# Layer norm and projections of an attention stage: some of ScalarE's time for z, another order on VectorE, projections in halves

## The chip, the cores and the metric

The kernel runs on the 8 cores of one Trainium2 chip. No core talks to another; each computes half of the rows of one of 4 sequences. The time is device microseconds of the slowest core, and the figure quoted is a median over runs.

## The reference

x is 4 sequences of 4096 rows with 1024 columns. Two pre-norm residual layers follow one another:

```
z   = layernorm(x)
q,k,v = z @ Wq, z @ Wk, z @ Wv            # 1024 -> 64 each
att = softmax(q @ k^T, axis=1)            # over the rows i of q, for each key column
x1  = x + tile(att @ v, 16)               # 64 -> 1024
z1  = layernorm(x1);  zp = z1 shifted by one row
r   = sigmoid((mu_r z1 + (1-mu_r) zp) @ Wr)
k   = (mu_k z1 + (1-mu_k) zp) @ Wk
y   = x1 + r * (relu(k)^2 @ Wv2)
```

The softmax runs over queries, so each key needs the exponentials of all 4096 queries. A core therefore makes z, q and k of all 4096 rows, and outputs only for its own 2048.

## The kernel before

Every engine has its program written out by hand, in a fixed order, with semaphores between them. The edited part is the first stage, which feeds the exponentials.

*Tiles and chunks.* The 4096 rows are 32 tiles of 128. x of a tile comes by DMA from SyncE's queue (`load_x`, line 327) into one of 8 slots. A slot is used again when z of the tile 8 before is made. VectorE computes the statistics of a tile with `stats(i)`: `stats_a` (first half, line 492), `stats_b` (second half, line 495, and the aggregate, line 497). GpSimd takes tiles in pairs: `scale` makes the negated mean, variance plus epsilon, and its power -0.5 for both (lines 402, 404, 407), and `apply` makes z = (x - mean) * rstd in bf16 for each (line 417). GpSimd counts tiles done in `G_Z`.

*z transposed.* Tiles 0 to 15 are transposed on TensorE (`T(i)`, line 810) into PSUM, and copied to `zT` by ScalarE for tiles 0 to 7 (`t_evac`, line 1122) and by VectorE for 8 to 15 (line 505). Tiles 16 to 31 are transposed by DMA from SyncE's queue (`turn_z`, line 336), in order with the loads of x.

*Chunk steps.* Four tiles are a chunk n of 512 rows, 0 to 7. `QK(n)` is the projection, 8 matmuls (line 827); `qk_evac(n)` on VectorE casts it to bf16 (line 510); `SW(n)` swaps the halves q and k on TensorE (line 839) and `sw_evac(n)` casts the result (line 514); `MX(n)` scores each key against a sample of 128 queries (line 851), and `mx(n)` takes the maximum as the shift of the exponential (line 528). For each two chunks `VP(sc)` projects the values (line 863, 16 matmuls), `v_evac` casts (line 518), `VT(sc)` transposes (line 873), `vt_evac` copies (line 522).

*Units.* A unit is a block of scores, 128 keys by 512 or 1024 queries. There are 136, numbered here from 0, in groups: a group may start when the swapped cast and the maximum of its chunk are there. Units 0 to 3 need chunk 0, 4 to 11 chunk 1, 12 to 19 chunk 2, 20 to 39 chunk 3, 40 to 47 chunk 4, 48 to 63 chunk 5, all others chunk 7. TensorE scores a unit with one or two matmuls (`fill`, lines 886 and 890) into a buffer in PSUM (2 buffers until unit 19, then 3), and ScalarE exponentiates it (`exps`, line 1139) and frees the buffer. `scores(n)` in TensorE's order means the next n units. From unit 64 on TensorE also adds up the output (line 899), between units.

The order of TensorE is a hand-written list in which `T`, `QK`, `SW`, `MX`, `VP`, `VT` and `scores` alternate; VectorE has a list of its own:

```
            mx(0)
            stats(10)
            stats(11)
            stats(12)
            t_evac(8)
            stats(13)
            qk_evac(1)
...
            v_evac(0)
            stats(15)
            qk_evac(2)
```

After the last exponential ScalarE loads the table of the square root (line 1148), and the second part follows: attention output, second layer norm (`ln2_apply`, line 1168, an Identity activation with a scale and a bias for each row), and the matmuls of the second layer (lines 1037, 1058, 1080).

Of the kernel before, what the change touches and what calls it, by code (L numbers as in the profile page):

```python
# [23 lines left out]
NA = 8  # L24
NF2 = 20
# [41 lines left out]
def build_program():  # L67
# [58 lines left out]
    with ctx:  # L126
# [12 lines left out]
        rstd = e(nc.sbuf_tensor("rstd", [128, TT], F32))  # L139
        so = e(nc.sbuf_tensor("so", [128, TOWN], F32))  # L140
# [108 lines left out]
        G_Z = sem("G_Z")  # L249
        P_T = sem("P_T")  # L250
# [45 lines left out]

        def own_p(kt):
            return P0[:, kt, :] if kt < 16 else Prot[:, kt % 4, :]
# [24 lines left out]
        def _(sy):  # L323
            def load_x(i):
                if i >= 8:
                    sy.wait_ge(G_Z, i - 7)
                sy.dma_start(out=xst[:, i % 8, :],
                             in_=x_in[i * 128:(i + 1) * 128, :]).then_inc(D_X[i % 8], 16)

            def turn_z(i):  # L330
                sc = i // 8
                sy.wait_ge(G_Z, i + 1)
# [59 lines left out]
        def _(g):  # L392
# [36 lines left out]
            g.wait_ge(G_Z, TT)  # L429
# [55 lines left out]
        def _(v):  # L485
# [56 lines left out]
            stats(12)  # L542
            t_evac(8)
            stats(13)
            qk_evac(1)
            t_evac(9)
            t_evac(10)
            sw_evac(1)
            mx(1)
            t_evac(11)  # L550
            stats(14)
            v_evac(0)
            stats(15)
            qk_evac(2)
            stats_a(16)
            vt_evac(0)
            mx(2)
            sw_evac(2)
            stats_b(16)
            t_evac(12)  # L560
            stats_a(17)
            t_evac(13)
            stats_b(17)
            t_evac(14)
            t_evac(15)
            stats(18)
            qk_evac(3)
            stats_a(19)
            sw_evac(3)
            mx(3)  # L570
            stats_b(19)
            stats(20)
            stats(21)
            v_evac(1)
            stats(22)
            vt_evac(1)
# [222 lines left out]
        def _(t):  # L799
# [3 lines left out]
            def T(i):  # L803
                t.wait_ge(G_Z, i + 1)
# [9 lines left out]
            def QK(n):  # L814
# [11 lines left out]
                for ct in range(CT):  # L826
# [4 lines left out]
                ins.then_inc(P_QK, 1)  # L831

            def SW(n):
                t.wait_ge(V_QK, n + 1)
                if n % 2:
                    t.wait_ge(V_SW, n)
                elif n:
                    t.wait_ge(V_VT, n // 2)
# [18 lines left out]
            def VP(sc):  # L857
                if sc == 0:
                    t.wait_ge(D_WV, 16)
                t.wait_ge(V_SW, 2 * sc + 2)  # L860
                for ct in range(CT):
# [52 lines left out]
            t.wait_ge(D_ID, 16)  # L914
            T(0)
# [11 lines left out]
            scores(2)  # L927
            QK(1)
# [3 lines left out]
            T(10)  # L932
            SW(1)
            MX(1)
            T(11)
            scores(1)
            VP(0)
            QK(2)
            scores(1)
            VT(0)  # L940
            scores(1)
            MX(2)
            SW(2)
# [4 lines left out]
            scores(1)  # L948
# [3 lines left out]
            scores(2)  # L952
            QK(3)
            scores(2)
# [3 lines left out]
            VP(1)  # L958
            scores(3)
            VT(1)  # L960
            scores(8)
            QK(4)
            scores(3)
# [3 lines left out]
            QK(5)  # L967
            scores(3)
# [3 lines left out]
            VP(2)  # L972
            scores(3)
            VT(2)
            scores(7)
            QK(6)
            scores(3)
            SW(6)
            MX(6)
            scores(3)  # L980
            QK(7)
            scores(3)
# [3 lines left out]
            VP(3)  # L986
            scores(2)
# [128 lines left out]
        def _(sc):  # L1116
# [25 lines left out]

            for i in range(NA):
                t_evac(i)
            for u_ in range(NU):
# [131 lines left out]
```

## Time and profile before

| | |
|---|---|
| median of 3 runs | 395.83 us (395.75 to 396.2) |
| profiled execution | 396.79 us, span of its slowest core 394.9 us |
| spans of the 8 cores | 388.7 to 394.9 us |
| TensorE busy | 312.6 us, 79% of the span |
| ScalarE busy | 225.9 us, 57% |
| VectorE busy | 224.5 us, 57% |
| GpSimd busy | 116.5 us, 29% |

The span runs from the first to the last instruction of a core. The shares are averages over parts with different limits: in the first 200 us ScalarE carries the exponentials, in the rest TensorE is busy nearly all the time. So the timelines and waits of the first part say more than the table. PE is TensorE, DVE VectorE, ACT ScalarE, POOL GpSimd.

### The profile page before, as it was taken

To read this page: it belongs to the slowest core of one execution; us is meant where nothing else is said; L and a number is where in the kernel's file an instruction comes from. 1 tells how busy PE (TensorE), PEld (TensorE's weight loads), DVE (VectorE), ACT (ScalarE), POOL (GpSimd) and SP (SyncE) were. 2 spreads that over 40 slices of the span, in tenths; PEclk is the share of its full clock that TensorE was granted. 3 is DMA by queue.
4 is the path that set the end of the run, shared out by engine and by line. 5 is a ranking of instruction groups with operands and counts; after the bars stand their busy time and mean duration, and the time that the engine had idled before them with its cause. 6 is when DMAs were issued, how large, how long until landed. Compare 5 with 4: busy or idle time off the path is not lost.

```text
span 394.9 us, 6253 instructions; the slowest of 8 cores (388.7 to 394.9 us)
## 1 busy us (share of the span) xinstructions
PE 312.6 (79%) x1938; PEld 143.1 (36%) x1938; DVE 224.5 (57%) x440; ACT 225.9 (57%) x354; POOL 116.5 (29%) x161
## 2 busy tenths in 40 slices
PE   0377986696878767776526989799999999999994
PEld 0333332231224434342223334244444444444441
DVE  2787789337236631112188976879278836781045
ACT  1252289989889999999916409302860267014610
POOL 1887457607304885068470021001000000000000
PEclk9997798866695888886555989899999999999999
DMA  7999547896596789991002004131322214130014
GB/s 179 291 317 287 144 140 188 147 290 102 101 173 188 250 176 181 183 266 79 1 2 46 7 2 81 27 147 67 55 53 106 110 33 75 69 144 2 0 53 160
DMA packets 42368, 48.58 MB, mean 123 GB/s; under 512 B 33248, under 2 KB 33504, under 8 KB 41952
## 3 DMA queue, kind: packets, MB, share of 16 engines
q1 hardware_dynamic: 41472, 41.44, 37.5%
q0 software_dynamic: 864, 6.75, 10.7%
q8 instruction: 16, 0.26, 0.3%
q14 instruction: 16, 0.13, 0.1%
HBM read 38.68 MB, written 8.39 MB: 119 GB/s over the span
## 4 chain that ended last, share of the span: by engine, by line
PE 52%; ACT 20%; DVE 12%; issue 11%; DMA 2%; POOL 1%; DVEq 0%; SPq 0%; ACTq 0%; POOLq 0%
PE F L1080 14%; PE F L1037 10%; PE F L1058 10%; PE tf L827 6%; PE F L886 6%; ACT Prot L1139 5%; ACT junkL L1139 5%; ACT junk L1139 4%; ACT P L1139 3%; DMA xst<-x_in 2%; DVE xr L667 2%; PE acc L899 2%; PE tf L863 1%; PE tx L810 1%; DVE dxk L677 1%
## 5 line engine op out<-in xcount | busy, mean ns | idle before, releaser
L886 PE MATMUL F<-qk 64*128 64x512 bf16 x136 | 59.2, 456 | 34.4 <-ACT Prot L1139 11.0
L1058 PE MATMUL F<-dxk,wk 128*128 128x512 bf16 x256 | 58.6, 386 | 1.8 <-DVE dxk L677 1.7
L1080 PE MATMUL F<-wv,ka 128*128 128x512 bf16 x256 | 57.5, 387 | 2.9 <-ACT ka L1186 2.9
L1178 ACT ACTIVATE rr<-F 128x1024 bf16<-128x1024 f32 x16 | 16.4, 1023 | 73.6 <-PE F L1037 73.6
L1037 PE MATMUL F<-wr,xr 128*128 128x512 bf16 x256 | 57.8, 384 | 0.6 <-DVE xr L667 0.6
L890 PE MATMUL F<-qk 64*128 64x512 bf16 x120 | 54.8, 474 | 0.0
L1139 ACT ACTIVATE P<-F,negm 128x1024 bf16<-128x1024 f32 (+1 forms) x40 | 37.2, 948 | 19.5 <-PE F L886 15.6
L1139 ACT ACTIVATE junk<-F,negm 128x1024 bf16<-128x1024 f32 x32 | 39.8, 1255 | 3.1 <-PE F L890 3.1
L1139 ACT ACTIVATE junkL<-F,negm 128x1024 bf16<-128x1024 f32 x32 | 39.9, 1281 | 0.0
L417 POOL TENSOR_SCALAR zst<-xst,nmean,rstd 128x1024 bf16<-128x1024 f32 x32 | 38.0, 1194 | 3.6 <-POOL rstd L407 3.6
L1139 ACT ACTIVATE Prot<-F,negm 128x1024 bf16<-128x1024 f32 x32 | 39.0, 1346 | 0.0
L1080 PEld LDWEIGHTS F<-wv,ka 128*128 128x128 bf16 x256 | 25.4, 99 | 34.5 <-issue 5.5
L1058 PEld LDWEIGHTS F<-dxk,wk 128*128 128x128 bf16 x256 | 25.3, 99 | 34.4 <-issue 6.1
L886 PEld LDWEIGHTS F<-qk 64*128 64x128 bf16 x136 | 12.4, 97 | 68.8 <-issue 66.4
L781 DVE TENSOR_TENSOR tmp<-F,rr 128x1024 f32<-128x1024 f32 x15 | 18.4, 1224 | 32.8 <-PE F L1080 32.5
L1037 PEld LDWEIGHTS F<-wr,xr 128*128 128x128 bf16 x256 | 25.2, 99 | 31.7 <-issue 2.7
L606 DVE TENSOR_REDUCE ell<-ellp 128x1 f32<-128x4 f32 (+1 forms) x32 | 4.9, 155 | 49.5 <-ACT junkL L1139 49.5
L439 POOL TENSOR_TENSOR fold<-x 128x512 f32<-128x512 f32 x16 | 20.2, 1265 | 33.9 <-DMA x<-x_in 33.9
L667 DVE SCALAR_TENSOR_TENSOR xr<-dxk,mu,z1T 128x256 bf16<-128x256 bf16 (+1 forms) x80 | 28.3, 427 | 2.3 <-PE F L1037 1.0
L492 DVE BATCH_NORM_STATS2 bnst<-xst 128x6 f32<-128x512 f32 x32 | 21.8, 680 | 8.3 <-DMA xst<-x_in 8.3
L827 PE MATMUL tf<-zT,wqk 128*128 128x512 bf16 x64 | 24.3, 549 | 1.4 <-ACT zT L1122 1.3
L810 PE MATMUL tx<-idsw,zst 128*128 128x128 bf16 x128 | 11.7, 249 | 17.1 <-POOL zst L417 15.9
(103 smaller groups left out, 446.7 us busy)
## 6 DMA issues: line engine op xcount, KB each, us to landing
xst<-x_in SPq DMA_DIRECT2D x32, 512.0 KB, 7.1
x<-x_in SPq DMA_DIRECT2D x16, 512.0 KB, 5.3
y_out<-x SPq DMA_DIRECT2D x15, 512.0 KB, 2.6
wr<-wr_in POOLq DMA_DIRECT2D x1, 2048.0 KB, 16.2
wk<-wk_in POOLq DMA_DIRECT2D x1, 2048.0 KB, 18.2
wv<-wv_in POOLq DMA_DIRECT2D x1, 2048.0 KB, 21.0
y_out<-x SPq DMA_DIRECT2D x2, 256.0 KB, 2.1
wqk<-wqk_in POOLq DMA_DIRECT2D x1, 256.0 KB, 9.2
```

What stands on the lines that cost most here:

```text
L417: g.tensor_scalar(zst[:, i % 8, :], xst[:, i % 8, :], nmean[:, i:i + 1], rstd[:, i:i + 1], ALU.add, ALU.mult).then_inc(G_Z, 1)
L439: g.tensor_tensor(fold[:, 0:512], x1[:, t_, 0:512], x1[:, t_, 512:1024], ALU.add).then_inc(G_XF, 1)
L492: v.bn_stats(bnst[:, i % 4, 0:6], xst[:, i % 8, 0:512]).then_inc(V_ST, 1)
L667: ins = v.scalar_tensor_tensor(xr[:, ct, o:o + w], dxk[:, q % 2, ct, o:o + w], mu[:, ct:ct + 1], z1T[:, ct, c0 - 1:c0 + w - 1], ALU.mult, ...
L781: v.tensor_tensor(tmp[:, :], F[(8 + j) % 3][:, :], rr[:, j, :], ALU.mult).then_inc(V_TMP, 1)
L827: ins = t.matmul(tf[0][:, :], wqk[:, ct, :], zT[:, (n // 2) % 2, ct, (n % 2) * 512:(n % 2 + 1) * 512], start=(ct == 0), stop=(ct == CT - 1 ...
L886: t.matmul(f[:, 0:512], qk2[0:64, kt * 128:(kt + 1) * 128], qk1[0:64, i0:i0 + 512], start=True, stop=True, skip_group_check=True, tile_pos ...
L890: t.matmul(f[:, 512:1024], qk1[64:128, kt * 128:(kt + 1) * 128], qk2[64:128, i0 + 512:i0 + 1024], start=True, stop=True, skip_group_check= ...
L1037: ins = t.matmul(f[:, hh * 512:(hh + 1) * 512], xr[:, ct, j * 128:(j + 1) * 128], wr[:, ct, hh * 512:(hh + 1) * 512], start=(ct == 0), sto ...
L1058: ins = t.matmul(F[k_ % 3][:, dd * 512:(dd + 1) * 512], wk[:, ct, dt * 128:(dt + 1) * 128], dxk[:, q % 2, ct, :], start=(ct == 0), stop=(c ...
L1080: ins = t.matmul(F[(8 + j) % 3][:, hh * 512:(hh + 1) * 512], ka[:, dt, j * 128:(j + 1) * 128], wv2[:, dt, hh * 512:(hh + 1) * 512], start= ...
L1139: sc.activation(dst, F[f_of[u_]][:, 0:w], AF.Exp, bias=negm[:, kt:kt + 1], accum_out=ellp[:, ell_col[u_]:ell_col[u_] + 1]).then_inc(A_EXP, 1)
```

## The change

- ScalarE makes z of tiles 5, 11 and 15, as one Identity activation with scale rstd and bias -mean * rstd. GpSimd makes that bias (`nmr1`) after the scale of the pair, and leaves out the tile. The new `z_done(i)` says which semaphore and count stand for z of tile i; all who waited on `G_Z` use it. ScalarE does tile 5 after its fourth copy, tile 11 after exponential 3, tile 15 after exponential 16.
- VectorE's order: the steps of chunks 1, 2 and 3 move ahead of later statistics, the first cast of the values moves behind statistics 15.
- TensorE's order: all projections but the first, and the value projections, are in two halves of 4 of the 8 steps, with one unit between (`QK2`, `VP2`); the units between other steps are spread anew.

```
+AZT = [5, 11, 15]
...
+        def z_done(i):
+            if i in AZT:
+                return A_Z, AZT.index(i) + 1
+            return G_Z, i + 1 - sum(a < i for a in AZT)
...
                 scale(2 * h, 2, h)
+                if 2 * h + 1 in AZT:
+                    i = 2 * h + 1
+                    g.tensor_tensor(nmr1[:, i:i + 1], nmean[:, i:i + 1], rstd[:, i:i + 1],
+                                    ALU.mult).then_inc(G_NM, 1)
                 apply(2 * h)
-                apply(2 * h + 1)
+                if 2 * h + 1 not in AZT:
+                    apply(2 * h + 1)
```

VectorE's order from `mx(0)` on, before and after:

```
 stats 10 11 12, t_evac 8, stats 13     | stats 10 11, qk_evac 1, t_evac 8
 qk_evac 1, t_evac 9 10                 | sw_evac 1, mx 1, t_evac 9 10 11
 sw_evac 1, mx 1, t_evac 11, stats 14   | stats 12 13, qk_evac 2, stats_a 14
 v_evac 0, stats 15, qk_evac 2          | sw_evac 2, mx 2, stats_b 14, stats 15
 stats_a 16, vt_evac 0, mx 2, sw_evac 2 | v_evac 0, t_evac 12 13, vt_evac 0
 stats_b 16, t_evac 12, stats_a 17      | stats 16, t_evac 14 15, stats 17
 t_evac 13, stats_b 17, t_evac 14 15    | qk_evac 3, stats_a 18, sw_evac 3
 stats 18, qk_evac 3, stats_a 19        | mx 3, stats_b 18, stats 19 20
 sw_evac 3, mx 3, stats_b 19            | v_evac 1, stats 21, vt_evac 1
 stats 20 21, v_evac 1, stats 22        | stats 22 ...
 vt_evac 1, stats 23 ...                |
```

Units that TensorE has scored before each step, before and after:

```
 QK 1: 3 | 2   QK 2: 5 | 7    QK 3: 14 | 18  QK 4: 29 | 31
 QK 5: 38 | 40 QK 6: 52 | 53  QK 7: 58 | 58
 VP 0: 5 | 11  VP 1: 18 | 22  VP 2: 42 | 44  VP 3: 62 | 62
```

The halves on TensorE, and ScalarE's part:

```
+            def QK2(n):
+                QK(n, 0, 4)
+                scores(1)
+                QK(n, 4, CT)
+            def VP2(sc):
+                VP(sc, 0, 4)
+                scores(1)
+                VP(sc, 4, CT)
...
+            def apply(i):
+                sc.wait_ge(G_NM, AZT.index(i) + 1)
+                if i >= 8:
+                    sc.wait_ge(P_T, i - 7)
+                sc.activation(zst[:, i % 8, :], xst[:, i % 8, :], AF.Identity,
+                              bias=nmr1[:, i:i + 1], scale=rstd[:, i:i + 1]).then_inc(A_Z, 1)
-            for i in range(NA):
+            for i in range(4):
                 t_evac(i)
-            for u_ in range(NU):
+            apply(5)
+            for i in range(4, NA):
+                t_evac(i)
+            for u_ in range(4):
+                exps(u_)
+            apply(11)
+            for u_ in range(4, 17):
+                exps(u_)
+            apply(15)
+            for u_ in range(17, NU):
                 exps(u_)
```

The waits of `VP`, `SW` and `T` on semaphores are fitted to the new order; what they wait for in data is the same.

## Rows read from the trace of the kernel before

**Rows 1.** Spans and granted clock of the cores (us, share of full clock).

```profile
core 0: 394.9 us, clock 0.868
...
core 2: 394.1 us, clock 0.881
...
core 5: 388.7 us, clock 0.892
```

**Rows 2.** ScalarE's waits, 29 to 121 us (us in total, times, longest).

```profile
ACT P L1139 <- PE F L886: 15.6, 5, 5.7
ACT P L1139 <- PE F L890: 3.8, 4, 1.7
ACT junk L1139 <- PE F L890: 3.1, 2, 1.7
```

**Rows 3.** Timeline of ScalarE (start us, us, engine, line, operation, count, idle before).

```profile
28.61 1.02 ACT L1122 ACTIVATE zT<-tx 128x1024 bf16<-128x1024 bf16 x1 [0.30 <-PE tx L810]
...
63.66 0.69 ACT L1139 ACTIVATE P<-F,negm 128x512 bf16<-128x512 f32 x1
...
76.69 1.12 ACT L1139 ACTIVATE P<-F,negm 128x1024 bf16<-128x1024 f32 x1
...
77.78 1.13 ACT L1139 ACTIVATE P<-F,negm 128x1024 bf16<-128x1024 f32 x1
...
111.41 1.10 ACT L1139 ACTIVATE junk<-F,negm 128x1024 bf16<-128x1024 f32 x1
...
195.93 1.28 ACT L1148 ACT_TABLE_LOAD   x1
```

**Rows 4.** Timeline of VectorE, 37 to 61 us.

```profile
37.33 0.67 DVE L510 CAST qk<-tf 128x512 bf16<-128x512 f32 x1
...
39.10 0.68 DVE L514 CAST qk<-tf 128x512 bf16<-128x512 f32 x1
39.70 0.68 DVE L528 TENSOR_REDUCE negm<-tf 128x4 f32<-128x512 f32 x1
...
48.90 0.69 DVE L514 CAST qk<-tf 128x512 bf16<-128x512 f32 x1
...
58.86 0.68 DVE L528 TENSOR_REDUCE negm<-tf 128x4 f32<-128x512 f32 x1
...
60.25 0.21 DVE L497 BATCH_NORM_AGGREGATE ag<-bnst 128x2 f32<-128x12 f32 x1
```

**Rows 5.** Timeline of TensorE, projections 1, 5 and 7.

```profile
30.75 3.13 PE L827 MATMUL tf<-zT,wqk 128*128 128x512 bf16 x8
...
80.79 3.59 PE L827 MATMUL tf<-zT,wqk 128*128 128x512 bf16 x8
...
106.30 3.55 PE L827 MATMUL tf<-zT,wqk 128*128 128x512 bf16 x8 [0.16 <-issue]
```

**Rows 6.** Timeline of GpSimd, 46 to 107 us.

```profile
46.93 0.23 POOL L402 TENSOR_SCALAR nmean<-ag 128x2 f32<-128x2 f32 x1 [5.37 <-DVE ag L497]
...
47.61 0.70 POOL L407 TENSOR_TENSOR rstd<-vpe,mhalf 128x2 f32<-128x2 f32 x1
48.56 2.37 POOL L417 TENSOR_SCALAR zst<-xst,nmean,rstd 128x1024 bf16<-128x1024 f32 x2 [0.24 <-POOL rstd L407]
...
106.13 0.62 POOL L432 DMA_DIRECT2D wr<-wr_in  x1 [3.85 <-DMA zT<-zst]
```

**Rows 7.** Timeline of TensorE on core 5, projections 3, 5 and 7.

```profile
50.59 1.90 PE L827 MATMUL tf<-zT,wqk 128*128 128x512 bf16 x8
...
77.27 3.11 PE L827 MATMUL tf<-zT,wqk 128*128 128x512 bf16 x8
...
101.67 1.89 PE L827 MATMUL tf<-zT,wqk 128*128 128x512 bf16 x8 [0.16 <-issue]
```

**Rows 8.** Timeline of ScalarE in the second part.

```profile
207.85 1.24 ACT L1168 ACTIVATE z<-x,nmr,rstd 128x1024 bf16<-128x1024 f32 x1 [0.65 <-DVE nmr L657]
...
218.13 1.28 ACT L1178 ACT_TABLE_LOAD   x1 [3.11 <-PE F L1037]
```

More of the change, by code:

```diff
@@ L249, in build_program @@
         G_Z = sem("G_Z")
+        G_NM = sem("G_NM")
+        A_Z = sem("A_Z")
         P_T = sem("P_T")
@@ L541, in _ @@
             stats(11)
-            stats(12)
+            qk_evac(1)
             t_evac(8)
-            stats(13)
-            qk_evac(1)
+            sw_evac(1)
+            mx(1)
             t_evac(9)
             t_evac(10)
-            sw_evac(1)
-            mx(1)
             t_evac(11)
-            stats(14)
+            stats(12)
+            stats(13)
+            qk_evac(2)
+            stats_a(14)
+            sw_evac(2)
+            mx(2)
+            stats_b(14)
+            stats(15)
             v_evac(0)
-            stats(15)
-            qk_evac(2)
-            stats_a(16)
+            t_evac(12)
+            t_evac(13)
             vt_evac(0)
[L557 to L563, printed above, removed]
+            stats(16)
             t_evac(14)
             t_evac(15)
-            stats(18)
+            stats(17)
             qk_evac(3)
-            stats_a(19)
+            stats_a(18)
             sw_evac(3)
             mx(3)
-            stats_b(19)
+            stats_b(18)
+            stats(19)
             stats(20)
+            v_evac(1)
             stats(21)
-            v_evac(1)
+            vt_evac(1)
             stats(22)
-            vt_evac(1)
             stats(23)
@@ L825, in QK @@
                     t.wait_ge(V_MX, n)
-                for ct in range(CT):
+                for ct in range(a, b):
                     ins = t.matmul(tf[0][:, :], wqk[:, ct, :],
@@ L855, in MX, with VP @@
                 ins.then_inc(P_MX, 1)
-            def VP(sc):
+            def VP(sc, a=0, b=CT):
                 if sc == 0:
                     t.wait_ge(D_WV, 16)
-                t.wait_ge(V_SW, 2 * sc + 2)
-                for ct in range(CT):
+                t.wait_ge(V_SW, 2 * sc + 2 if sc else 3)
+                for ct in range(a, b):
                     for h in range(2):
@@ L926, in _ @@
             T(7)
-            scores(2)
-            QK(1)
+            scores(1)
+            QK2(1)
             scores(1)
@@ L931, in _ @@
             T(9)
-            T(10)
             SW(1)
             MX(1)
+            T(10)
+            scores(2)
             T(11)
             scores(1)
-            VP(0)
-            QK(2)
+            QK2(2)
+            scores(2)
+            SW(2)
+            MX(2)
             scores(1)
[L940 to L943, printed above, removed]
+            VP2(0)
             scores(2)
@@ L947, in _ @@
             T(13)
-            scores(1)
+            VT(0)
+            scores(2)
             T(14)
@@ L951, in _ @@
             T(15)
-            scores(2)
-            QK(3)
-            scores(2)
+            QK2(3)
+            scores(1)
             SW(3)
@@ L957, in _ @@
             scores(2)
-            VP(1)
+            VP2(1)
             scores(3)
             VT(1)
-            scores(8)
-            QK(4)
-            scores(3)
+            scores(5)
+            QK2(4)
+            scores(2)
             SW(4)
@@ L966, in _ @@
             scores(6)
-            QK(5)
-            scores(3)
+            QK2(5)
+            scores(2)
             SW(5)
@@ L971, in _ @@
             scores(1)
-            VP(2)
-            scores(3)
+            VP2(2)
+            scores(2)
             VT(2)
-            scores(7)
-            QK(6)
-            scores(3)
+            scores(6)
+            QK2(6)
+            scores(2)
             SW(6)
             MX(6)
-            scores(3)
-            QK(7)
-            scores(3)
+            scores(2)
+            QK2(7)
+            scores(2)
             SW(7)
@@ L985, in _ @@
             scores(1)
-            VP(3)
-            scores(2)
+            VP2(3)
+            scores(1)
             VT(3)
```

18 lines of the change are left out of this document (10 added, 8 removed).

## The prediction

> **What bounds the kernel now.** I read the spans of the cores first. The slowest core sets the metric, and core 0 is slowest with 394.9 us; core 2 is close, core 5 is 6.2 us shorter [rows 1]. Next I looked for where core 0 changes its pace. ScalarE's timeline shows exponentials of full units 1.09 us apart (76.69, 77.78) and the table load that follows the last of 136 at 195.93 [rows 3]. The rest, 199.0 us on core 0, holds none of the edited lines and begins with that load. So the question is only when the last exponential ends: ScalarE's work in the first part is fixed, and what can be saved is its idle time. The waits of ScalarE from 29 to 121 us say how much there is: 15.6 + 3.8 + 3.1 = 22.5 us, all on score matmuls [rows 2]. Most of it lies before unit 20, the first that needs chunk 3, which is exponentiated at 63.66 [rows 3].
>
> Why scores are late is seen in the other engines. VectorE handles chunk 1 at 37.33 (cast), 39.10 and 39.70 (maximum), though its projection began on TensorE at 30.75 and took 3.13 us: statistics stand in front in VectorE's order [rows 4, 5]. GpSimd waits 5.37 us for the statistics of tiles 14 and 15, which stand behind such steps too, and starts that pair at 46.93 [rows 6]. From chunk 4 on there is a second loop. Statistics 26 to 31 stand behind projection 5 on VectorE; GpSimd makes their z; the DMA transposes it; projection 7 waits for that. On core 0 projection 5 ends at 80.79 + 3.59 = 84.38 and projection 7 starts at 106.30, 21.9 us later [rows 5]. On core 5 it is 77.27 + 3.11 = 80.38 to 101.67, 21.3 us [rows 7]. That the last transpose is the tight end is shown by GpSimd's weight load, which waits 3.85 us for it until 106.13, just before projection 7 [rows 6]. This loop has nothing to gain from a lead of ScalarE unless projection 5 itself ends earlier.
>
> **The change, step by step, core 0.** Start times before are rows, new ones my sums.
>
> *Tile 5 on ScalarE.* An application there costs 1.24 us by the layer-2 ones of the same shape [rows 8]. It falls between copies that wait for projection 0, so it costs nothing; without that cover it would cost its 1.24. GpSimd saves half of 2.37 us a pair and pays for one product 128x1. No row shows that product: it lies between the 0.23 of the negation and the 0.70 of the power, and I take 0.3, as it is the plainer operation [rows 6]. The saving, about 0.9, goes into waiting for the next statistics. Nothing is gained here.
>
> *Chunk 1.* Before, projection 1 stood behind two units, the second waiting for the first exponential, and began at 30.75. Now one unit stands in front and the copy of tile 7 (28.61 + 1.02) releases it: 29.7. With one unit inside (0.6) it ends at 33.4. The cast follows at once (37.33 before), then one copy; the swap comes behind transposes 8 and 9; the swapped cast starts at 35.6, the maximum at 36.2 instead of 39.70. Lead 3.5 us.
>
> *Chunk 2.* Transposes 10 and 11 with their copies put projection 2 at about 39.1; it ends near 42.0, as do statistics 12 and 13. Its swapped cast starts at 43.4 instead of 48.90 [rows 4]. Tile 11 on ScalarE lies in idle time. Lead over 5 us.
>
> *Chunk 3 gives part back.* Statistics 15 end at 47.0, no earlier than the 46.9, where GpSimd started on them before. GpSimd has z of 14 by 50.1, but tile 15 now stands in ScalarE's order behind exponential 16, which ends at about 51.8: z at 53.0, against 48.56 + 2.37 = 50.9 [rows 6]. Behind that wait stand transpose 15, its copy, projection 3. On SyncE's queue the load of x 23 waits for z 15 as well, 2 us longer, with the DMA transpose of tile 16 behind it; z of 16 comes after that anyway, and x 23 is wanted some 15 us later, so this costs nothing. The maximum of chunk 3 starts at 58.7, where it started before (58.86). The lead of the units remains, since units 0 to 19 need chunks 0 to 2 only: unit 20 at 59.4 instead of 63.66, 4.2 us.
>
> *Projection 4.* Before, the statistics of 18 were half done and those of 19 ended at 60.25 + 0.21, right after the maximum. Now both stand almost wholly behind it, and 19 is done at 61.7 [rows 4]. GpSimd needs 50.93 - 46.93 = 4.0 for the pair [rows 6], with 0.2 to start 65.9, and by the 3.85 of the last tile z lands at 69.7. Thirty-one units are scored by then; exponential 30 ends near 70.5 after about 0.7 lost on the split value projection. At 1.2 GHz, 0.45 us a matmul as in projection 5 (3.59 for 8), half a projection is 1.8 and a unit 0.6. So unit 31 comes at 72.1 and unit 32 at 74.3, against 76.69 [rows 3]. Of the lead 2.4 is left.
>
> *Projection 5* now follows 40 units, where it followed 38: 2 x 1.09 later in ScalarE's count. Exponential 36 ends at 74.3 + 5 x 1.09 = 79.8, one unit 0.6, the projection 3.6 with 0.6 for the unit inside: end 84.6, against 84.38. The whole lead is eaten at this point. The split itself saves little: ScalarE gets one more unit (1.09) while TensorE needs 0.6 more, 0.5 per projection at the low clock. At 2.4 GHz, 1.89 a projection, it saves nothing, since three buffered units cover that already.
>
> *Projection 7.* The loop of 21.9 less 0.3, as the swap stands behind two units now, puts its start at 106.2. Unit 59 is the second after its first half. Low clock: 106.2 + 3.6 + 1.2 = 111.0, against 111.41. High clock: 106.2 + 1.9 + 0.75 = 108.85. Then ScalarE runs to the end without gaps, as from 111.41 on before. The sum is -0.4 to -2.6 us. Core 0 had the low clock in projection 7, core 5 the high one [rows 5, 7], so I take -1.7. Core 2, 0.8 us ahead in span, I take to follow core 0.
>
> The profiled execution took 396.79 us with a span of 394.9, and lies 0.96 above the median of 395.83. A span of 393.2 then stands for 395.1 in its own time and **394.1 us** for the median.
>
> *A rule to weigh.* No row shows Identity while the exponential table is active; the rows show Identity in the layer-2 part with the next load only at 218.13, 1.28 us, before the sigmoid [rows 8]. The Trainium skill (ScalarE: Activation LUTs, "Table sets: the hidden batching unit") says that cheap functions are in every set; by that three applications cost no load, and the sum stands. Were it not so, six loads of 1.28, two of them in idle time, would add up to 5 us.
>
> **The rivals.**
> (A) As above: the loop 5 to 7 gives back the lead. -0.4 to -2.6, 393.2 to 395.4. Chance 0.45.
> (B) The clock is high in projections 4 and 5 (1.9 instead of 3.6). Then unit 32 comes at 72.3, projection 5 ends near 80.5, projection 7 starts near 102, and unit 59 comes 5 to 7 us earlier: 389 to 391; with one of the two high, 391.5 to 393. For it: denser work before chunk 3. Against it: 3.59 and 3.11 on both cores [rows 5, 7], with TensorE waiting between units. Chance 0.22. The Trainium skill (TensorE: Matmul & The Clock Gate, "What's actually happening") says that activity releases the throttle; the added wait for z before projection 4 speaks by that for (A).
> (C) The whole lead goes: core 2 or a core with late tiles comes out at its old end. 395.1 to 396.6. Chance 0.11.
> (D) Slower. Tile 15 waits on ScalarE and statistics 14 to 19 stand further back on VectorE. On a core that is early now this is loss. Core 5 begins projection 3 at 50.59 [rows 7]; by the same links as above I get exponential 16 done there at 50.2, z of 15 at 51.4, its transpose and copy by 52.9, so 2.3 us later, and the loop carries most of it to the end. If core 0 pays the same, the time is 395.83 + 2.2 - 0.5 = 397.5. It decides where projection 3 begins more than 3 us later than by my sum. For it: the chain through exponential 16 has six links in my sum (unit 16, its exponential, z, transpose, copy, projection), each of which can slip. Against it: on core 0 the old wait of 5.37 us goes. Chance 0.20, and 0.02 more for table loads.
>
> **How the numbers follow.** A difference under 0.2%, 0.8 us, can't be told from none. A puts some 0.13 of its chance within that; C 0.09, and 0.01 on either side. Faster 0.32 + 0.22 + 0.01 = 0.55; same 0.13 + 0.09 = 0.22; slower 0.01 + 0.20 + 0.02 = 0.23. The range leaves out the best half of B and the worst of D: 390.3 to 397.2; for A alone it is 393.2 to 395.4.
>
> **What would show it.** Right: the maximum of chunk 1 near 36, the swapped cast of chunk 2 near 44, that of chunk 3 unmoved; unit 20 four microseconds earlier; a wait of ScalarE and TensorE before projection 4 that was not there; projection 5 ending where it did; projection 7 released by the DMA. Wrong: projections 4 to 6 near 2 us each (B), projection 3 after 57 (D), a table load between 20 and 60 us, or a slowest core in which x arrives later than here.

## The result, and the profile after

The changed kernel takes **398.22 us** (median of 5 runs, 396.96 to 400.24) against 395.83 of before: ratio 1.006, 95% interval 1.0039 to 1.0081. The prediction, 394.1 us with a range to 397.2, was wrong. It went the way of rival D, the one that said slower. The profiled execution took 398.22 us too. Medians here and below are over all executions of a kernel; ratios, intervals and core means leave out the few in which one die showed a lower clock and took longer.

The spans of the cores (us, granted clock):

```profile
core 0: 396.4 us, clock 0.877
...
core 2: 395.4 us, clock 0.885
...
core 5: 393.1 us, clock 0.880
```

Core 0 is 1.5 us longer than in [rows 1], core 5 is 4.4 us longer. It is not a matter of the slowest core alone: the mean span of the eight cores over the runs went from 391.8 to 394.0. I call this mean the core mean below; it scatters less than the slowest core. For the kernel before it was 391.7 to 391.8 in each of the four groups of experiments below. The changed kernel was timed in five executions and not again in those groups, so differences of core mean against its 394.0 can be off by some 0.3.

ScalarE's waits on core 0, 29 to 122 us (us in total, times, longest):

```profile
ACT P L1167 <- PE F L904: 8.4, 8, 1.6
ACT P L1167 <- PE F L908: 7.6, 6, 3.8
ACT junk L1167 <- PE F L908: 2.8, 3, 1.5
ACT junkL L1167 <- PE F L908: 1.1, 1, 1.1
ACT Prot L1167 <- PE F L908: 0.5, 1, 0.5
```

That is 20.4 us of waits on scores, 2.1 less than the 22.5 in [rows 2]. But ScalarE now also does two applications of 1.23 in this stretch, 2.5 us. Waits that shrink because the engine does other work are no gain. ScalarE's timeline, to be held against [rows 3]:

```profile
35.29 1.23 ACT L1175 ACTIVATE zst<-xst,nmr,rstd 128x1024 bf16<-128x1024 f32 x1
...
52.24 1.23 ACT L1175 ACTIVATE zst<-xst,nmr,rstd 128x1024 bf16<-128x1024 f32 x1
...
62.98 0.69 ACT L1167 ACTIVATE P<-F,negm 128x512 bf16<-128x512 f32 x1 [1.32 <-PE F L904]
...
77.76 1.11 ACT L1167 ACTIVATE P<-F,negm 128x1024 bf16<-128x1024 f32 x1 [0.78 <-PE F L908]
...
111.72 1.11 ACT L1167 ACTIVATE junk<-F,negm 128x1024 bf16<-128x1024 f32 x1
...
118.75 1.12 ACT L1167 ACTIVATE junkL<-F,negm 128x1024 bf16<-128x1024 f32 x1 [1.10 <-PE F L908]
...
197.74 1.28 ACT L1192 ACT_TABLE_LOAD   x1
```

Unit 20 is 0.7 us earlier than before, not 4.2. Unit 32 is already 1.1 later. The table load comes 1.8 us later. Behind it 198.7 us are left, 199.0 before: all of the loss lies in the first part, as argued. VectorE shows where the lead went (compare [rows 4]):

```profile
36.59 0.69 DVE L529 CAST qk<-tf 128x512 bf16<-128x512 f32 x1 [0.31 <-PE tf L857]
37.20 0.68 DVE L543 TENSOR_REDUCE negm<-tf 128x4 f32<-128x512 f32 x1
...
44.34 0.69 DVE L529 CAST qk<-tf 128x512 bf16<-128x512 f32 x1
...
60.12 0.69 DVE L525 CAST qk<-tf 128x512 bf16<-128x512 f32 x1 [3.08 <-PE tf L842]
...
62.15 0.68 DVE L543 TENSOR_REDUCE negm<-tf 128x4 f32<-128x512 f32 x1
...
65.02 0.21 DVE L512 BATCH_NORM_AGGREGATE ag<-bnst 128x2 f32<-128x12 f32 x1
```

The maximum of chunk 1 is 2.5 us earlier, the swapped cast of chunk 2 is 4.6 earlier, the maximum of chunk 3 is 3.3 later. VectorE stood idle for 3.08 us before the cast of chunk 3, and the releaser is TensorE's projection. Statistics 19, behind it in order, end at 65.2, where they ended at 60.5. TensorE (compare [rows 5]):

```profile
53.72 1.01 PE L824 MATMUL tx<-idsw,zst 128*128 128x128 bf16 x8 [1.45 <-ACT zst L1175]
55.78 1.86 PE L842 MATMUL tf<-zT,wqk 128*128 128x512 bf16 x4 [1.05 <-DVE zT L520]
...
58.12 1.89 PE L842 MATMUL tf<-zT,wqk 128*128 128x512 bf16 x4
...
84.04 1.86 PE L842 MATMUL tf<-zT,wqk 128*128 128x512 bf16 x4 [0.16 <-issue]
86.38 1.46 PE L842 MATMUL tf<-zT,wqk 128*128 128x512 bf16 x4
...
108.95 1.02 PE L842 MATMUL tf<-zT,wqk 128*128 128x512 bf16 x4 [1.79 <-DMA zT<-zst]
110.23 1.04 PE L842 MATMUL tf<-zT,wqk 128*128 128x512 bf16 x4
```

Before, projection 3 on this core was:

```profile
54.83 1.90 PE L827 MATMUL tf<-zT,wqk 128*128 128x512 bf16 x8
```

Now it begins at 55.78, one microsecond later. But four of its matmuls take 1.86, where all eight took 1.90: it runs at 1.2 GHz. With the unit between its halves it lasts 4.2 us. On all eight cores it lasts 3.6 to 4.2 now and lasted 1.7 to 1.9 before. Ahead of projection 7 TensorE now waits 1.79 us for the DMA transpose, where [rows 5] has 0.16. GpSimd (compare [rows 6]):

```profile
48.19 0.23 POOL L412 TENSOR_SCALAR nmean<-ag 128x2 f32<-128x2 f32 x1 [1.03 <-DVE ag L512]
...
49.72 0.19 POOL L435 TENSOR_TENSOR nmr<-nmean,rstd 128x1 f32<-128x1 f32 x1
...
65.39 0.23 POOL L412 TENSOR_SCALAR nmean<-ag 128x2 f32<-128x2 f32 x1 [4.21 <-DVE ag L512]
...
109.25 0.65 POOL L447 DMA_DIRECT2D wr<-wr_in  x1 [3.86 <-DMA zT<-zst]
```

It waits for the statistics of tiles 18 and 19, and the last transpose of z is the tight end before projection 7, with the same 3.9 us. On core 0 projection 5 ends at 87.84 and projection 7 begins at 108.95: 21.1 us, where it was 21.9.

### The profile page after: what moved, and what is told of

The parts are those of the page before. It is cut to its first block, busy times and chain, and to the rows that moved or that the text cites. A ratio compares the mean times of both kernels' runs of the same rounds, so it can differ in the third digit from the quotient of the medians.

```text
span 396.4 us, 6290 instructions; the slowest of 8 cores (392.0 to 396.4 us)
## 1 busy us (share of the span) xinstructions
PE 311.4 (79%) x1938; PEld 142.1 (36%) x1938; DVE 223.9 (56%) x440; ACT 230.7 (58%) x357; POOL 113.6 (29%) x161
## 4 chain that ended last, share of the span: by engine, by line
PE 54%; ACT 17%; DVE 12%; issue 10%; DMA 3%; POOL 3%; SPq 1%; DVEq 0%; ACTq 0%; POOLq 0%
PE F L1108 13%; PE F L1086 13%; PE F L1065 10%; ACT junkL L1167 6%; PE tf L842 5%; PE F L904 4%; ACT Prot L1167 4%; PE tx L824 2%; DMA xst<-x_in 2%; DVE xr L681 2%; ACT P L1167 2%; ACT junk L1167 2%; POOL zst L427 2%; PE tf L881 2%; PE acc L917 2%
## 5 line engine op out<-in xcount | busy, mean ns | idle before, releaser
L904 PE MATMUL F<-qk 64*128 64x512 bf16 x136 | 57.6, 439 | 30.8 <-ACT junkL L1167 10.6
L1086 PE MATMUL F<-dxk,wk 128*128 128x512 bf16 x256 | 58.6, 386 | 1.6 <-DVE dxk L691 1.4
L908 PE MATMUL F<-qk 64*128 64x512 bf16 x120 | 52.3, 452 | 0.0
L427 POOL TENSOR_SCALAR zst<-xst,nmean,rstd 128x1024 bf16<-128x1024 f32 x29 | 34.4, 1193 | 3.0 <-POOL rstd L417 3.0
L842 PE MATMUL tf<-zT,wqk 128*128 128x512 bf16 x64 | 25.6, 548 | 7.5 <-DMA zT<-zst 3.2
L824 PE MATMUL tx<-idsw,zst 128*128 128x128 bf16 x128 | 13.1, 269 | 17.8 <-POOL zst L427 15.6
```

Of the source, the lines that this page charges most:

```text
L427: g.tensor_scalar(zst[:, i % 8, :], xst[:, i % 8, :], nmean[:, i:i + 1], rstd[:, i:i + 1], ALU.add, ALU.mult).then_inc(G_Z, 1)
L824: ins = t.transpose(tx[i % 2][:, ct, :], zst[:, i % 8, ct * 128:(ct + 1) * 128], ident)
L842: ins = t.matmul(tf[0][:, :], wqk[:, ct, :], zT[:, (n // 2) % 2, ct, (n % 2) * 512:(n % 2 + 1) * 512], start=(ct == 0), stop=(ct == CT - 1 ...
L904: t.matmul(f[:, 0:512], qk2[0:64, kt * 128:(kt + 1) * 128], qk1[0:64, i0:i0 + 512], start=True, stop=True, skip_group_check=True, tile_pos ...
L908: t.matmul(f[:, 512:1024], qk1[64:128, kt * 128:(kt + 1) * 128], qk2[64:128, i0 + 512:i0 + 1024], start=True, stop=True, skip_group_check= ...
L1086: ins = t.matmul(F[k_ % 3][:, dd * 512:(dd + 1) * 512], wk[:, ct, dt * 128:(dt + 1) * 128], dxk[:, q % 2, ct, :], start=(ct == 0), stop=(c ...
```

## Experiments

Four questions: which of the three parts costs time; whether the clock of projection 3 is the cause; whether the loop from projection 5 to projection 7 carries the loss to the end; and what is worth keeping. Kernels of one group ran on the same chip, and each has the median of the kernel before from there. The table has marks of six kernels, each the median over the eight cores, from the timelines (us): "P3" is the time from the first to the last matmul of projection 3, "max 3" the start of chunk 3's maximum, "P5 end" and "P7" the end of projection 5 and the start of 7, "load" the start of the table load that ends the first part. Each row is one profiled execution, so it holds some luck of that execution.

| kernel | P3 lasts | max 3 | P5 end | P7 | load |
|---|---|---|---|---|---|
| before | 1.9 | 56.5 | 82.2 | 103.8 | 192.0 |
| after | 3.9 | 58.9 | 85.6 | 106.8 | 195.6 |
| after, tile 15 on GpSimd | 2.3 | 56.1 | 83.3 | 104.4 | 193.6 |
| after, projection 5 two units earlier | 3.8 | 58.6 | 82.7 | 104.3 | 193.1 |
| orders alone | 3.3 | 57.5 | 83.4 | 104.6 | 192.8 |
| orders, projection 5 after 38 units | 3.0 | 57.2 | 80.8 | 102.9 | 191.0 |

### What each part costs

**Tile 15 back on GpSimd** (`e1_no15`).

```
-AZT = [5, 11, 15]
+AZT = [5, 11]
```

> The changed kernel with tile 15 back on GpSimd (AZT = [5, 11]). Theory 1, the queue: z of tile 15 stands behind exponential 16 on ScalarE (it was ready at 53.5, GpSimd would have it near 52.3), so projection 3 starts 1.2 us earlier, ScalarE saves 1.1, and the loop from projection 5 to 7 carries it: 1.0 to 1.5 us less than the changed kernel, some 396.8. Theory 2, the order of statistics alone makes chunk 3 late: no change, 398.2.

396.82 us against 396.02 (ratio 1.002, interval 1.0004 to 1.0035); core mean 392.9. So tile 15 alone costs 1.05 us of the core mean's 2.2. Projection 3 took 2.3 us on seven cores of eight and began 1.5 us earlier by the median of the cores, so theory 1 is borne out.

**No tile on ScalarE, orders and halves kept** (`e9_no_z`).

```
-AZT = [5, 11, 15]
+AZT = []
```

> The changed kernel with no z on ScalarE; new orders and halves stay. With tile 15 on GpSimd alone it was 1.4 us less. If tile 15 is the whole loss of that part, this gives the same, 396.8; if tiles 5 and 11 cost too, 396.2 or less.

397.06 against 395.91 (1.0025, 1.0007 to 1.0043); core mean 392.4. All three tiles together cost 1.55 of core mean, so tiles 5 and 11 cost some 0.5 beside tile 15.

**Whole projections** (`e2_whole`): the unit comes behind each projection, as before.

```
-                QK(n, 0, 4)
-                scores(1)
-                QK(n, 4, CT)
+                QK(n)
+                scores(1)
```

> The changed kernel with the projections whole and the unit of the middle behind each. Theory 1: the unit inside a projection delays what waits for the projection by 0.4 to 0.6 us each time, and ScalarE gets little for it: 0.5 to 1 us less than the changed kernel, 397.4. Rival: the halves are what keeps ScalarE fed while projections 4 to 6 run at the low clock; without them its idle time grows by 0.5 for each: 1 to 1.5 us more, 399.5.

398.76 against 396.02 (1.0068, 1.0053 to 1.0084); core mean 395.2, 1.2 above the changed kernel. Where z of three tiles is on ScalarE and the projections run slowly, the halves help.

**Halves alone, on the kernel before** (`e5_before_halves`): one of the units behind each projection moves between its halves, as below for one of them.

```
-            QK(1)
-            scores(1)
+            QK2(1)
```

> The kernel before with the halves alone: each projection that a score unit follows gets that unit between its halves; no z on ScalarE, no other order. My sum: at the low clock a split saves 0.5 us of ScalarE's idle time and delays the projection's users by 0.6; the loop from projection 5 to 7 loses 0.6, ScalarE wins 0.5: no change within 0.2%. Rival: the halves cost, 0.6 us in each of projections 3, 5 and 7 on the loop, +1 us or more over the kernel before.

396.86 against 395.96 (1.0017, 1.0 to 1.0035); core mean 392.6, 0.9 more than before: a small cost, just clear of the noise. Projection 3 went from 1.9 to 2.3 us at the high clock, since a unit now lies in it, and the maximum of chunk 3 waits for that. (Projection 3 also began 1.5 us later by the median of the cores; why was not followed.)

The price of the halves is plainest at the end. Unit 64, the first that needs chunk 7, comes behind projection 7, its swap, the value projection 3 and its transpose. The changed kernel on core 0, TensorE:

```profile
116.97 0.38 PE L891 MATMUL tb<-idsw,vT 128*128 128x128 bf16 x4 [0.65 <-DVE vT L533]
118.25 0.37 PE L904 MATMUL F<-qk 64*128 64x512 bf16 x1 [0.89 <-DVE v_sb L537]
```

ScalarE waits 1.10 us for that unit and starts it at 118.75, 9.80 us after projection 7 began. The kernel before on core 5, where projection 7 ran at the high clock too, begins it 9.03 us after the 101.67 of [rows 7], without a wait:

```profile
110.70 1.14 ACT L1139 ACTIVATE junkL<-F,negm 128x1024 bf16<-128x1024 f32 x1
```

The traces of all kernels agree: with projection 7 at the high clock it is 9.8 us on each of 70 cores with the halves and 8.9 to 9.0 on each of 36 without. Behind unit 64 all cores of all kernels take 79.0 to 79.2 us to the table load. So the two units inside projection 7 and the value projection 3 cost 0.8 us at the very end, wherever the rest of the halves may win it back. Halves everywhere but there were not tried.

**Orders alone** (`e6_order_only`): `AZT` empty and whole projections, all else as changed.

> The changed kernel with neither z on ScalarE nor halves: what is left is the new order on VectorE and TensorE (and the unit counts before each step). Order theory: this part alone makes it slower, because statistics 14 to 19 come later than before on most cores and projection 5 stands behind 40 units: +1.5 to +2.5 us over the kernel before. Queue theory: tile 15 on ScalarE is the loss, and this version is not slower than the kernel before.

396.14 against 395.96 (1.0011, 0.9992 to 1.003): no difference in the time that can be told; the core mean of 392.3 is some 0.65 above the kernel before. Against `e9_no_z` (392.4) the halves neither cost nor gain here. Projection 3 runs low on six cores of eight, so the low clock comes with the orders too, not with tile 15 only. Cores 1 and 7 had the same waits ahead of it, 1.27 us for an exponential and later 1.55 for the copy, and came out differently:

```profile
51.33 3.56 PE L842 MATMUL tf<-zT,wqk 128*128 128x512 bf16 x8 [1.55 <-DVE zT L520]
```

```profile
51.56 1.89 PE L842 MATMUL tf<-zT,wqk 128*128 128x512 bf16 x8 [1.55 <-DVE zT L520]
```

So the waits alone do not settle the clock of one core; some chance remains.

**z of three tiles on ScalarE, on the kernel before** (`e4b_before_z`): orders and projections as before; tile 15 stands behind exponential 9, where that order lets it.

```
-            for u_ in range(NU):
+            apply(5)
...
+            for u_ in range(4, 10):
+                exps(u_)
+            apply(15)
+            for u_ in range(10, NU):
```

> The kernel before with only z of tiles 5, 11 and 15 on ScalarE; both orders as before. Tile 15 stands behind exponential 9 here, since that order scores 12 units before it transposes tile 15. Queue theory: ScalarE does 3.4 us more, 1.1 of it while it is fed, and z of 15 is hardly earlier than by GpSimd: 0 to +1 us over the kernel before. Rival: GpSimd's work was a bound of the first stage, then 1 us or more less than the kernel before.

399.72 against 395.96 (1.0096, 1.0077 to 1.0115), the slowest of all; core mean 395.2. The three tiles are the costliest part: +3.5 of core mean here, +2.9 between orders alone (392.3) and whole projections with the tiles (395.2), +1.6 between `e9_no_z` and the changed kernel. What a part costs depends on the slack that the others leave. Added in one order they do make up the whole: orders +0.65 (`e6_order_only`), tiles +2.85 (`e2_whole`), halves -1.2, together 2.3 of core mean.

### The clock of projection 3

**More work for TensorE before it** (`e10_busy`): the eight transposes of tile 14 are done four times over, with the same output. Nothing else differs from the changed kernel.

```
-                for ct in range(CT):
+                for ct in [c for _ in range(4 if i == 14 else 1) for c in range(CT)]:
```

> The changed kernel, but the eight transposes of tile 14 are done four times over on TensorE (same source, same place, same values), so that it computes while it waits for z of tile 15. No data comes earlier. Clock theory: in the changed kernel projection 3 ran at the low clock on all eight cores (3.6 to 4.2 us) and at the high one before (1.9); with the gap filled it is at the high clock (2.3) on most cores, the maximum of chunk 3 starts 1.3 to 1.9 us earlier, and the time is 1 to 1.5 us less than the changed kernel. Rival: the clock isn't decided by this gap; projection 3 stays at 3.6 to 4.2 us and the time stays, or rises by the added work.

The stretches around projection 3 on core 3 (us from:to, length, busy us and instructions of each engine, granted clock, DMA share, GB/s); first the changed kernel, then this one:

```profile
46.00:50.00 4.00, 2.10 (x23) 1.13 (x20) 3.24 (x7) 3.68 (x8) 1.42 (x3) 1.00 0.68 220
50.00:53.00 3.00, 1.75 (x11) 0.89 (x12) 1.98 (x4) 1.05 (x2) 0.00 (x0) 0.62 0.65 217
53.00:56.00 3.00, 3.00 (x8) 0.53 (x6) 0.11 (x1) 1.21 (x2) 2.26 (x4) 0.50 0.00 0
```

```profile
46.00:50.00 4.00, 3.35 (x46) 2.46 (x44) 3.12 (x6) 3.69 (x10) 2.15 (x4) 1.00 0.74 194
50.00:53.00 3.00, 1.83 (x24) 1.20 (x22) 1.90 (x4) 2.03 (x3) 0.00 (x0) 1.00 0.61 168
53.00:56.00 3.00, 2.37 (x12) 0.64 (x10) 1.73 (x5) 1.71 (x3) 1.39 (x4) 1.00 0.40 162
```

TensorE's first entry rises from 2.10 to 3.35 of 4 us, and the clock stays at 1.00 where it fell to 0.62 and 0.50. The kernel before, as long ahead of its projection 3 (50.93 on this core), was as busy as that:

```profile
45.00:49.00 4.00, 3.44 (x38) 1.97 (x36) 3.88 (x8) 3.69 (x7) 2.03 (x2) 1.00 0.50 144
```

TensorE's timeline of `e10_busy` on core 3:

```profile
48.69 1.95 PE L824 MATMUL tx<-idsw,zst 128*128 128x128 bf16 x32 [0.65 <-POOL zst L427]
51.08 0.61 PE L824 MATMUL tx<-idsw,zst 128*128 128x128 bf16 x8
52.73 1.02 PE L842 MATMUL tf<-zT,wqk 128*128 128x512 bf16 x4 [1.05 <-DVE zT L520]
54.01 1.04 PE L842 MATMUL tf<-zT,wqk 128*128 128x512 bf16 x4
```

It starts projection 3 at 52.73, 0.87 later than the changed kernel (51.86), and ends it at 55.05, 1.04 earlier (54.20 + 1.89 = 56.09). The high clock was there on all eight cores. In time it was less clear: 398.43 against 395.91 (1.0059, 1.0028 to 1.0089, 7 runs), core mean 393.1, that is 0.85 lower while the slowest core was not. In the profiled execution the two slowest cores (1 with 397.8 and 0 with 395.9) are the two on which projection 7 ran at the low clock (3.8 and 3.7 us), which it did on no core of the changed kernel; the other six have 391.4 to 393.7.

**The same again** (`e16_busy_again`), the same kernel on another chip.

> The changed kernel with the repeated transposes of tile 14, once more on another chip, for the mean over all cores and not the slowest alone. Clock theory: the mean span of the cores is 0.8 to 1.5 us below that of the changed kernel (393.98 in its five executions), with projection 3 at 2.3 us on all cores. Rival: the mean is that of the changed kernel.

397.05 against 395.94 (1.0024, 1.0007 to 1.004); core mean 392.7; again projection 3 high on all eight cores. Over both runs a high clock there is worth 0.85 to 1.2 us of core mean, about half of the loss, with the time of the added transposes already taken off.

**Tile 15 earlier in ScalarE's order** (`e11_z15_early`), behind exponential 13 in place of 16.

```
-            for u_ in range(4, 17):
+            for u_ in range(4, 14):
                 exps(u_)
             apply(15)
-            for u_ in range(17, NU):
+            for u_ in range(14, NU):
```

> The changed kernel with z of tile 15 behind exponential 13 on ScalarE instead of 16. Queue theory: it is ready up to 2 us earlier (ScalarE reaches it while GpSimd's bias is just there), the gap before transpose 15 closes, projection 3 begins 1 to 2 us earlier and at the high clock: 1.4 to 2.5 us less than the changed kernel, as good as tile 15 on GpSimd. Rival: the cost is the 1.1 us of ScalarE's own time, then it stays at 398.

398.19 against 395.91 (1.0047, 1.0024 to 1.0071); core mean 393.1, 0.9 lower than the changed kernel. Projection 3 ran high on six cores, low on cores 5 and 7, and these two were the slowest of the profiled execution: 396.6 and 397.3 us, the others 391.1 to 393.7. Their projection 1 ran low as well (4.2 us for 2.3), so the gap is not the price of projection 3 alone. Both the mean and the slowest core follow the clock here.

### Statistics behind chunk 3, and the loop

**Statistics 17 and 18 ahead of projection 3's cast** (`e7_fill`), to use VectorE's idle 3.08 us.

```
-            t_evac(15)
             stats(17)
+            t_evac(15)
+            stats(18)
             qk_evac(3)
-            stats_a(18)
+            stats_a(19)
...
-            stats_b(18)
-            stats(19)
+            stats_b(19)
```

> The changed kernel with statistics 17 ahead of the copy of tile 15, and statistics 18 ahead of the cast of chunk 3, in time in which VectorE waits (1.8 and 3.1 us). Order theory: z of tiles 16 to 23 comes 2 to 4 us earlier. Where projection 4 waits for the transpose this saves up to 1 us; on core 0 it didn't wait. 0 to 1 us less than the changed kernel. Rival: late z of 16 to 23 is what is lost, then 2 us or more less.

397.89 against 396.02 (1.0046, 1.0026 to 1.0067); core mean 393.6, 0.4 lower. Projection 5 ended where it had (85.6 by the median of the cores, with the edit and without). The place of these statistics is not what holds projection 5.

**Projection 5 two units earlier** (`e3_q5early`): it follows 38 units, as before the change.

```
-            scores(6)
+            scores(4)
             QK2(5)
...
             VT(2)
-            scores(6)
+            scores(8)
```

> The changed kernel with projection 5 after 38 units, as before the change, instead of 40, and two more units ahead of projection 6. Loop theory: projection 5 is released by ScalarE's pace, so it ends 2.2 us earlier, projection 7 (which waits for the DMA transpose) starts up to 2.2 us earlier, and the end moves by 1.5 to 2.2: 396.3. Rival: the end is set by the units alone, no change.

396.8 against 396.02 (1.0031, 1.0003 to 1.006); core mean 392.8, 1.2 lower. In the table projection 3 is as slow as in the changed kernel and chunk 3 as late (58.6), but projection 5 ends 2.9 us earlier (2.0 by its start; on three cores it also ran at the high clock, 2.3 us), projection 7 starts 2.5 earlier and the table load comes 2.5 earlier. The loop carries what projection 5 gains to the end of the first part, with little lost on the way.

**The same on the kernel before** (`e14_before_q5`): projection 5 after 36 units.

```
-            scores(6)
+            scores(4)
             QK(5)
...
-            scores(7)
+            scores(9)
```

> The kernel before with projection 5 after 36 units instead of 38 and nothing else. Loop theory: the loop from projection 5 to 7 also bounds the kernel before, so this alone gains 1 to 1.5 us. Rival: before the change ScalarE's stream and the loop were balanced, so an earlier projection 5 gives nothing, and the gain of the version with the new orders came with the lead of the first chunks.

395.66 against 395.94 (0.999, 0.9974 to 1.0006): no difference. Projection 5 ended 1.5 us earlier by the median of the cores (80.65), and projection 7 began at 103.9 as ever. It was not z that held it. GpSimd's weight load, which waits for the last transpose of z, and projection 7 on core 5:

```profile
99.86 0.62 POOL L432 DMA_DIRECT2D wr<-wr_in  x1 [3.92 <-DMA zT<-zst]
```

```profile
101.53 1.89 PE L827 MATMUL tf<-zT,wqk 128*128 128x512 bf16 x8 [0.16 <-issue]
```

On all eight cores z was there 1.5 to 2.5 us before projection 7 began. Projection 7 stood behind its 58 units, and these come at ScalarE's pace of 1.09 us. In the kernel before, the two ends meet: the weight load lies within 0.3 us of the start of projection 7 on every core. So the rival of the expectation holds: ScalarE's stream and the loop were balanced, and one of them moved alone gives nothing. In the changed kernel TensorE waits 1.65 to 1.9 us for z before projection 7 on every core, and there the loop does bind.

### What is worth keeping

**Three repairs on the changed kernel** (`e8_fill_no15_q5`): the edits of `e1_no15`, `e3_q5early` and `e7_fill` together.

> The three repairs together on the changed kernel: tile 15 on GpSimd, projection 5 after 38 units, statistics 17 and 18 in VectorE's waiting time. Each measured alone gave about 1.4, 1.4 and 0.3 us. If they add up: 3 us less than the changed kernel, 395.2, half a microsecond or more below the kernel before. If the first two buy the same thing (projection 5 earlier): 396.8, as each alone.

395.61 against 395.96 (1.0006, 0.9988 to 1.0023); core mean 392.1. It comes back to the kernel before and not past it.

**Orders alone, with the moved statistics and the earlier projection 5** (`e13_order_q5`): the edits of `e6_order_only`, `e7_fill` and `e3_q5early`.

> Only the new orders, with projection 5 after 38 units and statistics 17 and 18 in VectorE's waiting time; no z on ScalarE, no halves. The orders alone were level with the kernel before (ratio 1.001). If the loop from projection 5 to 7 bounds it as in the changed kernel, projection 7 starts 2 us earlier and this version is 1 to 1.5 us faster than the kernel before, 394.7. If ScalarE's own stream bounds it by then, no gain: 396.1.

394.48 against 395.91 (0.996, 0.9943 to 0.9977); core mean 390.0, 1.8 under before.

**The same without the moved statistics** (`e15_order_q5_nofill`): `AZT` empty, whole projections, and

```
-            scores(6)
+            scores(4)
             QK2(5)
...
             VT(2)
-            scores(6)
+            scores(8)
```

> The orders alone with projection 5 after 38 units, without the moved statistics 17 and 18. That pair of edits together gave 1.4 us less than the kernel before. If projection 5 is what counts, 394.7; if it needs z of tiles 20 to 23 earlier as well, it waits for the transposes and stays at 395.5 or more.

**393.29** against 395.94 (0.9932, 0.9914 to 0.9949, 6 runs), 0.7% faster than the kernel before and the fastest of all; core mean 389.7. The orders alone have 392.3, the earlier projection 5 alone 391.4 (`e14_before_q5`), both together 389.7, with 391.8 before: the gain comes with both together. TensorE's timeline on core 0:

```profile
51.84 3.04 PE L842 MATMUL tf<-zT,wqk 128*128 128x512 bf16 x7 [1.77 <-DVE zT L520]
...
77.73 3.59 PE L842 MATMUL tf<-zT,wqk 128*128 128x512 bf16 x8
...
103.10 1.89 PE L842 MATMUL tf<-zT,wqk 128*128 128x512 bf16 x8 [0.16 <-issue]
```

Projection 3 is slow here too (3.04, one of its eight matmuls is missing from the records). Projection 5 ends at 81.3, 3.1 before that of [rows 5], and projection 7 begins 3.2 before. ScalarE's table load shows the same:

```profile
191.15 1.28 ACT L1187 ACT_TABLE_LOAD   x1
```

It was at 195.93 in [rows 3].

## Why the prediction was wrong

**The frame held.** Only the end of the last exponential matters: 198.7 us follow the table load against 199.0. The loop holds as well: 21.1 us on core 0 for my 21.6. I called it the tight end in the kernel before; `e14_before_q5` shows that ScalarE's pace was as tight there.

**Where the sum went off.** The sum took 1.7 us off the span of core 0 and the span grew by 1.5, 3.2 us apart. Projection 7 began 2.75 us late (108.95 for 106.2), by the slip at chunk 3 below. Behind unit 59 came 1.5 us that the sum had at nothing. The part behind the table load gave 0.3 back, and the high clock of projection 7, where I took a value between the two, gave 0.85: that was luck. Small remainders make up the rest.

**Tile 5, the product, the tables.** The product took 0.19 (I took 0.3), an application 1.23 (1.24), and no table load stands between the exponentials: that term of nothing was right. That tiles 5 and 11 cost nothing is not borne out: together they cost some 0.5 of core mean. The larger cost is tile 15's, by who waits for it.

**Chunks 1 and 2.** My leads of 3.5 and over 5 us came out as 2.5 and 4.6. Near enough, and of little use, since `e6_order_only`, which has the lead without the other parts, gains nothing by it. On core 0 projection 1 ran at the low clock, as it had for most of its 3.13 us before, and as my sum kept it; on six of the other cores it took 2.3 us in place of the 4.2.

**The step that failed: "Chunk 3 gives part back."** I put its maximum at 58.7; it came at 62.15. My sum implied a start of projection 3 at about 54.7 (58.7 less the 4.03 between the two of before) and kept its 1.90 us, the length of before. It began at 55.78 and lasted 4.2. Of the 3.4 us, 1.1 is the later start (z of tile 15 at 53.47 for 53.0, then the links behind it) and 2.3 the length: 1.9 from the low clock, 0.4 from the unit between the halves (2.3 where `e1_no15` ran high). I had asked about the clock for projections 4, 5 and 7, and never for 3. The row that needed it was there: 1.90 for eight matmuls means 2.4 GHz, a thing that can be lost.

What TensorE did before the clock fell, on core 3: from 46 to 50 us it was busy for 2.10 of 4 us, with most of a wait of 1.46 us for z from ScalarE in that stretch, and then it waited 1.05 for the copy. In `e10_busy`, with 3.35 of 4 us busy, the first wait filled and the same wait of 1.05, the clock stayed. The Trainium skill (TensorE: Matmul & The Clock Gate, "What's actually happening") says that activity releases the throttle; the two runs with more transposes agree, on all sixteen cores. I had used that sentence for the wait before projection 4, one wait too late.

**Projections 4 and 5** then follow my sums, moved by this slip. Statistics 19 end at 65.2 for my 61.7, and projection 4 begins 8.0 us behind them in my sum (69.7) and on the chip (73.2). My sum for projection 5, moved by 3.4, gives an end of 88.0; it was 87.84. That the clock stayed low in both, against rival B, was right. `e3_q5early` shows the last link: with chunk 3 as late as ever but projection 5 two units earlier, 2.5 of the 3.6 us at the table load come back.

**The second step that failed: "Then ScalarE runs to the end without gaps."** Projection 7 ran at 2.4 GHz. By my formula unit 59 comes at 108.95 + 1.9 + 0.75 = 111.6; it was 111.72. But the halves push the steps of the last chunk back, and ScalarE waits 1.10 us before its unit 64, a wait that was not there before. From unit 59 to the table load it is 86.0 us for 84.5. This is 1.5 us of the miss, and `e5_before_halves` and `e9_no_z` have the same wait of 1.1 on core 0, while `e2_whole` and `e6_order_only`, without the halves, have none.

**The rival that came true, and not by its own condition.** D asked for projection 3 to begin over 3 us later than by my sum; it began 1.1 later and ended 3.4 later. The price D gave, 397.5, is 0.7 under the measured 398.22.

**The halves.** I had them save 0.5 per projection at the low clock: it is 1.2 of core mean with the tiles on ScalarE, from all projections together. On the kernel before, where projection 3 runs high, they cost 0.9. That they saved nothing at the high clock was right; I took their cost there as nothing too, and that was wrong: 0.4 in projection 3, and 0.8 from the start of projection 7 to unit 64.

**What stays open.** The low clock of projection 3 is not the whole loss: making it high gives 0.85 to 1.2 of the 2.2 us of core mean. `e6_order_only` has it low on six cores and costs 0.65; its projection 3 is whole, and nothing in front of it waits for z from ScalarE. How the rest divides is not shown. A later start of projection 3 has little of it: its mean over the cores is 53.0 before and 53.1 after, and core 0, with 0.95, is not typical. Why the moved statistics help a little in `e7_fill` (0.4 of core mean) and cost in `e13_order_q5` (0.3 of core mean against `e15_order_q5_nofill`, on another chip) I can't say; both are near the noise.

The slowest core tells of something else as well. In the 17 profiled executions projection 1 ran wholly or partly at the low clock on 46 of 136 cores. On these the table load came 1.25 us later than the mean of their execution, on the others 0.6 earlier, and in 12 of the 17 the slowest core was one of them; core 0 of the changed kernel is one, with 4.2 us. This is seen and not tried: no run changes the clock of projection 1 alone, and why it falls on some cores is open.

## What to carry to other kernels

Before giving a piece of a chain to an idle engine, ask where it stands in that engine's order: z of tile 15 behind exponential 16 took 1.2 us off GpSimd and cost 1.05 us of mean span. Before moving one bound step, see what else ends at the same time: in the kernel before, ScalarE's pace and the last transpose met within 0.3 us, and projection 5 moved up alone gave nothing. A matmul group that runs at the high clock is an asset with a price of its own (here 1.9 us): each new wait ahead of it has to be weighed against the loss of that clock. A lead that an order gains pays only when the next bound step in the loop is moved up with it: orders alone gained nothing, with projection 5 moved up they gave 0.7%. A unit put inside a group delays all that waits for the group's end: 0.8 us for two such units ahead of unit 64.

## What the runs showed of the hardware

- After idle times of only 1.46 and 1.05 us (core 3), with TensorE busy for 2.10 of the 4 us from 46 to 50, its clock stood at half for the next projection, on all eight cores (3.6 to 4.2 us for 2.3 with the halves). Twenty-four more transposes of 128x128, 1.95 - 0.61 = 1.34 us of work, kept it high on all eight, in two runs. Equal waits need not give equal clocks: on cores 1 and 7 of `e6_order_only` projection 3 took 3.56 and 1.89 us behind the same waits of 1.27 and 1.55.
- Identity activations ran with no table load: on core 0 one among the copies and two among the exponentials, and no load between those at 1.47 and 197.74 us.
- A GpSimd product of 128x1 takes 0.19 us, less than the 0.23 of the negation of 128x2.
